# Five of sixteen states of a selective scan kept in columns in turns 2 and 3, beside a mixture-of-experts block, on one Trainium2 core

## The reference, cut to what matters

```python
u = silu(conv(in_proj(ctx)))                       # columns: channel on the partition, time along the row
delta = softplus(dt_proj(x_proj(u)[:16])); B, C = x_proj(u)[16:32], x_proj(u)[32:]
for n in range(16):                                # per channel
    state_n[t] = state_n[t-1] * exp(delta[t]*A[n]) + delta[t]*u[t]*B[n][t]
y[t] = sum over n of state_n[t] * C[n][t] + D * u[t]
x1 = x + tanh(g_xattn) * y * silu(layernorm(x))
out = x1 + tanh(g_ffn) * (ffn(xn, Ws) + sum over e of w_e * ffn(xn, W[e]))    # xn = layernorm(x1)
ffn(x, W) = (silu(x @ W1) * (x @ Wg)) @ W2
```

## Time and profile before

| | us |
|---|---|
| median of 3 runs | 1383.5 (1383.01 to 1387.35) |
| the profiled execution, its own time | 1382.22 |
| span of its records | 1380.2 |
| PE busy | 1330.0 (96%) |
| DVE busy | 967.9 (70%) |
| ACT busy | 626.9 (45%) |
| POOL busy | 430.6 (31%) |
| mean granted clock of PE | 0.994 |

### The profile page before, as it was taken

How to read it: one execution, slowest core, us unless ns; L and a number is a source line. 1 busy time by engine, 2 the same in 40 slices (tenths; PEclk the granted TensorE clock), 3 DMA queues, 4 the chain that set the end, 5 groups by cost and what they waited for, 6 DMA issues and landing times.

```text
span 1380.2 us, 17947 instructions
## 1 busy us (share of the span) xinstructions
PE 1330.0 (96%) x6178; PEld 1049.8 (76%) x6178; DVE 967.9 (70%) x1106; ACT 626.9 (45%) x1024; POOL 430.6 (31%) x237
## 2 busy tenths in 40 slices
PE   7899799999999999999999999999999999999999
PEld 4455467777777878888888878888888888888887
DVE  5999867899999766688988766688988722121111
ACT  6888466666556235544354235544354122111111
POOL 0000545788889411222333111122333111111111
PEclk8999999999999999999999999999999999999999
DMA  7211676777667855554455755554455655555552
GB/s 228 82 56 61 207 282 244 275 258 250 231 222 273 287 187 175 191 181 162 152 193 199 274 186 175 192 180 162 153 192 199 213 198 195 186 182 182 182 184 90
DMA packets 90796, 266.43 MB, mean 193 GB/s; under 512 B 11472, under 2 KB 11600, under 8 KB 90336
## 3 DMA queue, kind: packets, MB, share of 16 engines
q1 hardware_dynamic: 85408, 258.26, 53.7%
q10 hardware_dynamic: 5312, 7.16, 1.5%
HBM read 207.58 MB, written 57.80 MB: 192 GB/s over the span
## 4 chain that ended last, share of the span: by engine, by line
PE 82%; DVE 12%; ACT 3%; issue 2%; DMA 0%; POOL 0%; ACTq 0%; DVEq 0%
PE ps_hg L484 23%; PE ps_h L484 20%; PE ps_y L484 16%; PE ps_y L654 8%; PE ps_mid L561 7%; DVE st L1215 5%; PE ps_h L553 2%; DVE y_rows L1221 2%; ACT dA L869 1%; PE ps_mid L525 1%; PE ps_hg L553 1%; PE ps_y L553 1%; DVE st L1206 1%; DVE u L1124 1%; DVE u L1112 1%
## 5 line engine op out<-in xcount | busy, mean ns | idle before, releaser
L1517 POOL TENSOR_TENSOR h_lo<-h_tmp,h_hi 128x512 fp32r<-128x512 f32 x128 | 256.8, 2006 | 725.8 <-ACT h_hi L944 663.6
L484 PE MATMUL ps_h<-x_hi,w_split 128*128 128x512 f32 x1024 | 345.2, 399 | 1.5 <-DVE x_lo L1291 1.2
L484 PE MATMUL ps_hg<-x_hi,wg_split 128*128 128x512 f32 x1024 | 345.0, 398 | 0.8 <-DVE h_tmp L1362 0.8
L1215 DVE TENSOR_TENSOR_SCAN st<-dA,st 128x1024 f32<-128x1024 f32 x128 | 306.2, 2402 | 0.0
L1362 DVE TENSOR_TENSOR h_tmp<-h_tmp,ps_hg 128x512 f32<-128x512 f32 x128 | 88.1, 688 | 293.7 <-PE ps_hg L484 289.9
L484 PE MATMUL ps_y<-w_split,h_hi 128*128 128x512 f32 x1024 | 255.1, 396 | 0.1
L944 ACT ACTIVATE h_hi<-h_tmp 128x512 fp32r<-128x512 f32 x128 | 80.6, 630 | 343.1 <-DVE h_tmp L1362 343.1
L484 PEld LDWEIGHTS ps_h<-x_hi,w_split 128*128 128x128 f32 x1024 | 192.3, 188 | 41.6 <-issue 2.1
L484 PEld LDWEIGHTS ps_hg<-x_hi,wg_split 128*128 128x128 f32 x1024 | 192.3, 188 | 40.5 <-issue 1.2
L484 PEld LDWEIGHTS ps_y<-w_split,h_hi 128*128 128x128 f32 x1024 | 187.9, 188 | 38.0 <-ACT h_hi L944 0.6
L938 ACT ACTIVATE h_tmp<-ps_h 128x512 f32<-128x512 f32 x128 | 76.2, 595 | 286.8 <-PE ps_h L484 286.7
(11 more groups left out here) (154 smaller groups left out, 1119.2 us busy)
## 6 DMA issues: line engine op xcount, KB each, us to landing
w_split<-split_scratch SPq DMA_DIRECT2D x192, 512.0 KB, 4.9
wg_split<-split_scratch SPq DMA_DIRECT2D x96, 512.0 KB, 4.4
split_scratch<-w_split SPq DMA_DIRECT2D x64, 512.0 KB, 4.7
b_all<-xd_scratch SPq DMA_DIRECT2D x64, 256.0 KB, 4.1
split_scratch<-wg_split SPq DMA_DIRECT2D x32, 512.0 KB, 3.2
w_raw<-in_W_dram SPq DMA_DIRECT2D x14, 1024.0 KB, 7.4
wg_raw<-in_Wg_dram SPq DMA_DIRECT2D x7, 1024.0 KB, 8.9
dA<-in_x_dram SPq DMA_DIRECT2D x4, 1024.0 KB, 7.6
```

The costliest lines, as they stand in the source:

```text
L484: mm = pe.matmul(out_, lhs[a], rhs[c], start=first and q == 0, stop=last and q == len(sides) - 1)
L1215: dve.tensor_tensor_scan(flat[1], flat[0], flat[1], 0.0, ALU.mult, ALU.add).then_inc(scan_done, 1)
L1517: pool.tensor_tensor(h_lo[:, j, :], h_tmp[j % 2][:], h_hi[:, j, :].bitcast(F32), ALU.subtract).then_inc(hl_ready, 1)
```

## The change

In turns 2 and 3 (`late(m)`) the states 0, 3, 6, 9 and 12 (`COLS`) are no longer transposed one by one. DVE multiplies such a state in columns by C (`scale_columns`: two instructions of 128x1024, with C's row broadcast to all partitions by a DMA, `load_c`), GpSimd adds the result to `y_cols` (`column_state`: four instructions of 128x512), and `y_cols` is transposed once at the end (`columns_to_rows`) and added to `y_rows` (`add_columns`). `y_cols` starts as D times u, so that the four `init` places go away. `y_cols` and C's rows lie where the raw weights lay. The list of bank uses is written anew for these turns.

Two more pieces: at the start of turn 0 x_proj is moved ahead of a wait on PE, ACT's `front_xd` ahead of four scalings, ACT's `stage(1, 1)` behind the first decays, and DVE's statistics ahead of `front_dt_low`; in batch 0 the convolution's first two taps stand at place 0, its third at place 1, ACT's silu of u comes one tile earlier, and what follows on DVE moves up by one place.

The diff, cut to its core:

```diff
+        y_cols = w_raw[0]
+        c_all = [w_raw[1][:, i, :] for i in range(2)]
+        LATE_FRONT = [name for name in FRONT if not name.startswith("init")]
+        COLS = list(range(0, DS - 1, 3))
+        ROWS = [n for n in range(DS) if n not in COLS]
+            return len(front_names(m)) + T * ROWS.index(n) + (2 * i if n == DS - 1 else i)
+        def cols_place(m, i):
+            return sum_place(m, DS - 1, i) + 1
...
             def state_to_rows(m, n, i):
+                if late(m) and n in COLS:
+                    return
+            def columns_to_rows(m, i):
+                bank, before = mid(m, cols_place(m, i))
+                pe.wait_ge(col_added, T * NC * (m - 1))
+                mid_free(bank, before)
+                for et in range(T):
+                    mm = pe.transpose(ps_mid[bank][:, et * P:(et + 1) * P], y_cols[:, et, i * P:(i + 1) * P], ident[:])
+                mm.then_inc(mid_done[bank], 1)
...
                     if 0 <= n < DS:
                         state_to_rows(m, n, g % T)
+                        if late(m) and n == DS - 1:
+                            columns_to_rows(m, g % T)
...
+            front(0, "xproj")
             pe.wait_ge(dt_w_low, 1)
-            front(0, "xproj", "dt0", "dt1", "dt2", "dt3", "ccols")
+            front(0, "dt0", "dt1", "dt2", "dt3", "ccols")
...
+                if late(m) and n - 2 in COLS:
+                    dve.wait_ge(col_added, T * (NC * (m - 2) + COLS.index(n - 2)) + 2 * h + 2)
...
+            def scale_columns(m, n, h):
+                dve.wait_ge(scan_done, 2 * (DS * m + n) + h + 1)
+                dve.tensor_tensor(st[odd][:, two], st[odd][:, two],
+                                  c_all[used % 2].rearrange("p (a l) -> p a l", a=1).broadcast_to([P, 2, L]),
+                                  ALU.mult).then_inc(col_scaled, 1)
             def sum_rows(m, n, i):
+                if late(m) and n in COLS:
+                    if i < 2:
+                        scale_columns(m, n, i)
+                    return
+            def add_columns(m, i):
+                dve.tensor_tensor(y_rows[:, i, :], y_rows[:, i, :], ps_mid[bank][:], ALU.add).then_inc(mid_read[bank], 1)
             def slot(m, n, r):
                 elif 1 <= n <= DS:
                     sum_rows(m, n - 1, r - 1)
+                    if late(m) and n == DS:
+                        add_columns(m, r - 1)
...
-                    late = 2 if b == 0 else 0
-                    if late and p < late:
-                        front_conv(m, (p,))
+                    late = 1 if b == 0 else 0
+                    if late and p == 0:
+                        front_conv(m, range(DC - 2))
...
+            def column_state(m, k, part):
+                for et in (part, part + 1):
+                    pool.wait_ge(col_scaled, 2 * used + part // 2 + 1)
+                    pool.tensor_tensor(y_cols[:, et, :], y_cols[:, et, :], st[odd][:, et, :], ALU.add).then_inc(col_added, 1)
+                    for e in range(2, NE):
+                        step_(STEPS * b + e, ahead=lambda j: column_state(m, e - 2, 2 * j) if j < 2 else None)
```

More of the change, by code:

```diff
@@ L215, in gated_block @@
         ud_ready = sem("ud_ready")
+        cc_ld = [sem(f"cc_ld{i}") for i in range(2)]
+        col_scaled = sem("col_scaled")
+        col_added = sem("col_added")
         first_sum = sem("first_sum")
@@ L263, in mid @@
                 return bank, FIRST_BANKS[:place].count(bank)
[L264 removed]
+            return place % 2, 1 + place // 2 + MID_FIRST[place % 2] + turns(m - 1)
         def taken(m, place):
@@ L271, in mid_router @@
         def mid_router(b, place):
-            return place, MID_FIRST[place] + MID_TURN // 2 * b
+            return place, MID_FIRST[place] + turns(b)
         def front_names(m):
-            return FRONT if some(m) else FIRST_FRONT
+            return LATE_FRONT if late(m) else FRONT if some(m) else FIRST_FRONT
         def front_place(m, name):
@@ L689, in between @@
                     if m is not None:
-                        front(m, *{5: ("xproj", "init0"), 6: ("dt0", "init1"), 7: ("dt1", "ccols"), 8: ("dt2", "init2"),
-                                   9: ("dt3", "init3"), 10: ("z0", "z1")}.get(g, ()))
+                        names = {5: ("xproj", "init0"), 6: ("dt0", "init1"), 7: ("dt1", "ccols"), 8: ("dt2", "init2"),
+                                 9: ("dt3", "init3"), 10: ("z0", "z1")}.get(g, ())
+                        front(m, *[name for name in names if name in front_names(m)])
                 if some(b):
@@ L972, in after @@
                     if j == 0:
-                        if some(b) and m is not None:
+                        if m is not None:
                             front_silu(m)
@@ L1073, in _ @@
             decays(0, 0, T)
+            stage(1, 1)
             stage(1, 2)
@@ L1192, in front_du @@
                 if some(m):
-                    dve.wait_ge(*taken(m, front_place(m, "init3")))
+                    dve.wait_ge(*((ud_ready, T * m) if late(m) else taken(m, front_place(m, "init3"))))
                 else:
@@ L1228, in slot @@
                         sum_rows(m, n - 2, T - 1)
+                        if late(m) and n - 2 == DS - 1:
+                            add_columns(m, T - 1)
                 elif 1 <= n <= DS:
                     sum_rows(m, n - 1, r - 1)
+                    if late(m) and n == DS:
+                        add_columns(m, r - 1)
                 if n < DS:
@@ L1259, in make_y @@
                 for i in tiles:
-                    bank, before = mid(m, sum_place(m, DS - 1, i))
+                    bank, before = mid(m, cols_place(m, i) if late(m) else sum_place(m, DS - 1, i))
                     dve.wait_ge(mid_read[bank], before + 1)
@@ L1567, in _ @@
             batch(0, 1)
-            with pool.Fori(1, NB - 1) as b:
+            for b in range(1, NB - 1):
                 batch(b, b + 1)
```

69 lines of the change are left out of this document (55 added, 14 removed).

## The result

The changed kernel takes 1420.5 us (median of 4 runs, 1420.01 to 1421.69), the kernel before beside it 1384.8: a ratio of **1.0253**, 95% interval 1.0238 to 1.0269. That is slower, as forecast, but by 36 us and not by 18; 1420.5 lies above the range. The profiled execution has a span of 1419.0 against 1380.2, and PE's mean granted clock (the share of its full clock that the chip let PE have) is 0.975 instead of 0.994.

What follows compares the result with a forecast made beforehand. PE was taken as the bound with DVE close behind. Turn 0 -2.0, turn 1 0, step 0 -5.8, middle steps +13.2 and step 7 +12.4 gave +17.8: 1400.0 us, 1401.3 against the median; range 1384 to 1413.

Steps and rivals of the forecast that it cites:

- The middle steps: Steps 2 to 6 of turns 2 and 3, ten in all: +1.32 us a step, +13.2, with DVE held by POOL.
- the holding: Middle steps: three POOL instructions make DVE wait 1.15, 1.15 and 0.45 us before the scan ends.
- The rule that POOL and DVE take turns: With two SBUF inputs they exclude each other; POOL follows the running DVE instruction, the next on DVE waits some 1.1 us.
- Transposes at 17.53, `gate(2)` at 18.18: Place 4 of a middle step, from PE's first group: `gate(2)` starts at 18.18 instead of 16.86 us, +1.32.
- slack left: Middle step: product 2 at 21.0 us, distances then as before, DVE about 1.1 idle before product 0, so delay doesn't grow.
- a sign to look for: Place 4 of a middle step: PE idle some 4 us, where it was 0.57.
- E: Rival, middle steps: one block more of holding a step, DVE's 1.1 us of slack used up; +29.6, 1413 us; chance 0.10.
- Step 7: Step 7 of turns 2 and 3: pieces wait for reads of the one bank they use; +6.2 us a turn, +12.4.
- At place 0 the column piece waits for the last sum of state 14, +0.7: Step 7, place 0: the wait lasts as long as one sum on DVE (0.74 us); +0.7 a turn.
- Steps 0 and 1: Step 0 of turns 2 and 3: `init` places and the wait of `ccols` go; -2.9 us a turn, -5.8.
- Turn 0 and turn 1: Turn 0: x_proj and DVE's chain come earlier, -2.0 us; turn 1: later first product against ACT's shorter wait, 0.
- C's rows: Ten DMAs of 256 KB on SP, behind the fetches they follow, with nothing later waiting: 0 us.

Runs made afterwards that it cites:

- experiment 1: Changed kernel with 13 idle matmuls on PE at place 4 of the ten middle steps, ahead of the wait for the scan: 1401.7 us.
- experiment 5: Changed kernel with step 7's transposed columns in the free down-projection banks and state 15's pieces alternating between the two middle banks: 1412.8 us.
- experiments 1 and 6: The second of these is the changed kernel with both the 13 idle matmuls at place 4 and the free banks in step 7: 1392.9 us.
- experiment 7: Kernel before with only the change's reorderings: turn 0's alone 1384.5 us (0.9995), turn 0's and turn 1's together 1381.6 us (0.9977).
- the last run of experiment 8: Changed kernel with only D u in columns, free banks in step 7, and 38 instead of 20 idle matmuls ahead of turn 1: 1378.3 us (0.9949).
- experiment 4: Changed kernel with 13 idle matmuls at place 4 and the additions to D u on DVE instead of POOL: 1416.8 us.
- experiment 3: Changed kernel with each of POOL's 40 additions covering one column of 512, so y is not computed: 1382.1 us.

## Why the prediction missed

**The middle steps: the holding right, the price of the idle time missing.** +13.2 was forecast and +35.0 measured: 12.8 are the holding, 19.6 the clock, and 2.7 stand at the end of the two steps 6 and belong to step 7. The holding was walked to 0.1 us (products at 5.61 and 14.0, measured 5.60 and 13.95), and with the clock kept a step is 40.58 where 40.6 was forecast: +1.28 against +1.32. The rule that POOL and DVE take turns, read from the taps, holds in this step: one POOL instruction gets in behind each DVE instruction with two SBUF inputs. The step that failed is the sentence behind it, "Transposes at 17.53, `gate(2)` at 18.18", with "product 2 comes at 21.0: slack left". `gate(2)` did begin there (18.20), but it was priced at some 2.8 from rows of a PE that had been busy until then; it took 5.06 or 4.11, and product 2 came at 23.7. I had worked out an idle time of some 4 us for PE and listed it as a sign to look for, and asked only whom it makes late, not what it does to PE itself. It costs 1.5 or 2.7 a step, 19.6 in the ten by the distances of products, 18.8 by the times of experiment 1. That is the size of the miss (1401.3 against 1420.5). That the rest fits to 1 us is in part luck: the kernel before took 1384.8 beside the result and not 1383.5, and the errors of the small terms below go both ways. None of the rivals had it; E, the one on the far side, had one block more of holding, and there was none.

The kernel before has the sign of it too. In its own trace PE is idle for 4.74 at the end of turn 0, and behind it the granted clock is 0.64 in 166 to 170; the prediction looked at no such stretch. The Trainium skill (TensorE: Matmul & The Clock Gate, Why this matters for your kernels) says that long idle gaps of PE between bursts of matmuls bring back the lower clock. The trace agrees for one of 3.78; the prediction drew on that page for the transposes and not for this.

**Step 7: right.** Forecast +6.2 a turn; measured +5.4 in step 7 and 1.35 at the end of step 6, 6.8. With free banks 3.9 of it a turn went away by the time of experiment 5, and 4.7 by the steps of experiments 1 and 6, in which the clock doesn't move. The idle times at places 1 and 3 were 1.51, each with 0.16 to follow. "At place 0 the column piece waits for the last sum of state 14, +0.7" was the term too small: it is the 1.35.

**Steps 0 and 1: right.** -2.9 a turn forecast, -3.2 and -3.3 measured; `ccols`, which waited 0.59, waits no more.

**Turn 0 and turn 1: -2.0 together forecast, -3.2 by the ratio of experiment 7 and -3.9 by its medians** (1.8 to 4.7 gained). Turn 0 alone brought at most 2. In turn 1 ACT's wait of 2.83 for the logits is 0.30 in the changed kernel and in the last run of experiment 8. That this comes of DVE's normalization, which left the place behind product 3, fits the order of the code; no run tried it by itself.

**C's rows** were costed at 0 and nothing in the steps waits for them. **A place of transposes at 0.50** is borne out: from product 3 to the next product 0, where one place fell away and PE waits for nothing, it is 18.75 instead of 19.24.

## What to carry over

When a change makes a busy engine wait in one place, price what comes behind the wait as well: on PE a single idle time of some 4 us cost another 1.5 to 2.7 us at the lower clock, more than the 1.3 by which the step had become late. A delay of 2.3 us that fell into three pieces cost nothing of the kind; whether it was spared because it was shorter or because it was split was not tried. Where the idle time can't be removed, idle matmuls in it bring the clock's part back (18.8 us here), but not the wait itself. And moving the additions from DVE to POOL relieved DVE of only a third of their cost here: those that fell ahead of product 1 held DVE.

## What the runs showed of the chip

- **PE's granted clock.** Behind a single idle time of 3.78 (changed kernel) or 4.16 (four idle multiplications) it fell to 0.50 in each of the ten steps, for part or all of the transposes and of the next 12 matmuls, which took 4.11 or 5.06 instead of 2.76 in the changed kernel. Behind 0.70, 0.38 and 1.19 in one step it stayed at 1.00. Behind 1.89 it fell in two steps of ten (experiment 4), and behind 1.51 in step 7 of one turn and not of the other (experiment 3), each time with the same work. So what an idle time does is not settled by its length alone. What decides in between was not tried.
- **The same idle time can go either way.** Behind 4.74 us at the end of turn 0 the clock was back at 1.00 by 170 in one trace and at 0.50 until after 174 in another of the same order, and product 0 came 2.8 later behind x_hi. That this is what parts the quicker executions of the kernel before from the others, some 3 us, is argued from their mean clocks (0.994 against 0.990 and 0.991).
- **Transposes follow the clock as well**: four of them lasted 0.60 to 0.66 at 1.00 and 1.11 at 0.50.
- **POOL and DVE.** With both engines queued, a POOL addition of 128x512 took 2.7 on the mean, and DVE's multiplication of 128x1024 took 2.25 instead of 1.22. One column wide, the addition no longer held the multiplication (1.20). With four additions a step, POOL relieved DVE of 1.0 of 3.2 us.
